# Slot attention in a decoder block: a new order for VectorE and ScalarE in the first part of an iteration

## The chip, the cores and the metric

The kernel runs on one core of a Trainium2 chip. The metric is the device time of one execution in microseconds (us), median over runs. Five engines work side by side and meet at semaphores: TensorE (PE in the profile; PEld is its weight load), VectorE (DVE), ScalarE (ACT), GpSimd (POOL) and SyncE (SP), which issues transfers. Each engine works off its own instructions in the order in which they are written, so an instruction that waits holds up all that stand behind it on its engine.

## The reference

The block has three parts: decay attention with an MLP, cross-attention with three rounds of slots and a GRU, and a routed mixture of experts. Only the second is touched. Its core, with 2048 slots of width 256 and 1601 context rows:

```python
k_proj = einsum('bmd,ed->bme', Pn, Wk);  v_proj = einsum('bmd,ed->bme', Pn, Wv)
for _ in range(3):
    sn = rmsnorm(slots, slot_norm_w)
    q = einsum('bkd,ed->bke', sn, Wq)
    scores = einsum('bkd,bmd->bkm', q, k_proj) * scale
    attn = softmax(scores, axis=-2)                      # over the slots
    attn = attn / (sum(attn, axis=-1, keepdims=True) + EPS)
    updates = einsum('bkm,bmd->bkd', attn, v_proj)
    slots = gru_cell(updates, slots, gru_wi, gru_wh, gru_bi, gru_bh)
```

## The kernel before

Everything of this part is in `cross_attention`, one program written out by hand for each engine, with a loop over three iterations `it`. The keys and queries are folded beforehand, so that scores are the context (`kq_hi`, `kq_lo`) times the slots (`s_hi`, `s_lo`). Numbers are held as a rounded part and a remainder (`hi`, `lo`), and each product is three matmuls (`three_pass`, lines 76 to 78).

The 1601 context rows make 13 tiles `m` (`MT`), of 128 rows each but the last, which has 65. The 2048 slots make four chunks `c` of 512 columns. A score block (m, c) is six matmuls of 512 columns into one PSUM bank. In the main loop two banks are used in turn (`score_bank`), so a block may start only when the block two places before has been read out. The first four tiles (`AHEAD`) are the `lead`: their 16 blocks have an order of their own, and PE uses three banks there.

What happens to a tile:

- **scaling** (VectorE, L838, `scale_scores`): reads the bank, multiplies, writes `x_e` (chunks 0 to 2) or `x_E` (chunk 3) and takes a maximum. It frees the bank. `negated` (L844) then gives the tile's maximum to ScalarE.
- **exponentials** (ScalarE, L766 for chunks 0 to 2, L768 for chunk 3), with their sums.
- **inverse** (VectorE, L855 and L856, two tiny instructions), which waits for both exponentials.
- **normalised copies** (ScalarE, L771 for chunks 0 to 2, L772 for chunk 3), which wait for the inverse.
- **high parts** (ScalarE, L749 into `p_hi`, one for each of chunks 0 to 2) and **low parts** (VectorE, L850 into `p_lo`). A high part of tile m waits until the update of tile m-2 has read the slot that it takes.
- **sums** (VectorE, L868, for tile 0 the copies L865): they add the tile to `x_acc`, chunks 0 to 2 at once (`sum_weights(m, 0)`) and chunk 3 (`sum_weights(m, 1)`).
- **update** (PE): six matmuls for each chunk 0 to 2, with `p_lo` and `p_hi` as moving data. They need the low part.

PE's order in the main loop is: four score blocks of tile m, then the three updates of tile m-4. After the scores of tile 12 come the updates of tiles 8 to 12, then in a tail the updates of chunk 3 for all tiles, with the row sums (`x_acc` times ones, L1047) after the third of them.

`e` holds four tiles, so the scaling of (m, 0) waits for the sum of tile m-4 and for its last low part. On VectorE, before, `tile_lo(m)` puts a tile's two sums and three low parts in one piece, behind all four scalings of a later tile. The inverse of tiles 1 to 3 comes late: that of tile 2 behind `tile_lo(1)`, that of tile 3 behind `tile_lo(2)` and ahead of `tile_lo(3)`. On ScalarE each tile goes exponentials, both copies, high parts; the same holds for the last two.

## Time and profile before

| | us |
|---|---|
| median of 3 runs | 1453.31 |
| lowest, highest | 1444.6, 1454.62 |
| the profiled execution | 1452.9 |
| its span | 1451.2 |
| PE busy | 1259.7 (87%) |
| VectorE busy | 917.4 (63%) |
| ScalarE busy | 688.9 (47%) |

The profile is a record of one execution. Times within it count from the start of the span. The part that the change touches stands in it three times, roughly at 325 to 500, 568 to 742 and 810 to 984 us. A pause in square brackets is idle time of the engine right before an instruction, with what ended it. The ends of matmuls are modelled, so that neighbouring rows overlap; the distance between two starts is what one of them costs.

### The profile page before, as it was taken

What the parts mean: (1) busy time and instruction counts of PE and PEld (TensorE: products, weight loads), DVE (VectorE), ACT (ScalarE), POOL (GpSimd) and SP (SyncE); (2) the same over time, 40 slices, a digit from 0 to 9 for tenths busy, and PEclk for the clock granted to TensorE, in tenths of its full rate; (3) what the DMA queues carried; (4) which work ended last, traced back from release to release, by engine and by line L of the source; (5) the groups of instructions that cost most, each with busy time, mean ns of one, the idle gap of its engine ahead of it and who ended that gap; (6) DMA issues with size and microseconds to landing.
All of it is one profiled execution on the core that took longest, in us unless ns stands there. A gap on an engine that the chain in (4) does not pass through costs nothing. (4 is left out here: it accounts for less than half of the span.)

```text
span 1451.2 us, 19688 instructions
## 1 busy us (share of the span) xinstructions
PE 1259.7 (87%) x6374; PEld 1043.4 (72%) x6374; DVE 917.4 (63%) x2022; ACT 688.9 (47%) x1219; POOL 291.7 (20%) x366
## 2 busy tenths in 40 slices
PE   3898799659899999989999989999963999999960
PEld 3456688437687788767787868778753999999960
DVE  4325766456786466777546777745466777777747
ACT  4112323154567333656643366653341777777734
POOL 5703200020000000000000000000004566666633
PEclk9999899778999999999899989989955999999985
DMA  5000000500000100000000000006091111111134
GB/s 194 1 0 1 0 19 26 173 20 1 1 0 1 30 8 16 1 1 1 0 30 16 8 1 0 1 15 247 1 342 51 38 43 43 43 43 43 43 121 133
DMA packets 44904, 63.73 MB, mean 44 GB/s; under 512 B 7136, under 2 KB 35745, under 8 KB 44449
## 3 DMA queue, kind: packets, MB, share of 16 engines
q1 hardware_dynamic: 38148, 48.00, 10.1%
q0 software_dynamic: 4416, 12.06, 2.7%
q10 hardware_dynamic: 2272, 2.81, 0.5%
q8 instruction: 37, 0.61, 0.2%
q14 instruction: 31, 0.25, 0.1%
HBM read 50.47 MB, written 12.39 MB: 43 GB/s over the span
## 5 line engine op out<-in xcount | busy, mean ns | idle before, releaser
L76 PE MATMUL x_psum<-x_s_lo,x_kq_hi 128*128 128x512 f32 (+1 forms) x312 | 131.9, 423 | 23.1 <-DVE x_mx L838 21.3
L707 POOL TENSOR_TENSOR x_sq<-x_sq 128x512 f32<-128x512 f32 x12 | 15.5, 1289 | 617.2 <-ACT x_sq L693 617.2
L76 PE MATMUL x_psum<-x_p_lo,x_v_hi 128*128 128x512 f32 (+1 forms) x312 | 130.3, 418 | 3.6 <-DVE x_p_lo L850 3.6
L78 PE MATMUL x_psum<-x_p_hi,x_v_hi 128*128 128x512 f32 (+1 forms) x312 | 128.9, 413 | 0.0
L77 PE MATMUL x_psum<-x_p_hi,x_v_lo 128*128 128x512 f32 (+1 forms) x312 | 128.9, 413 | 0.0
L77 PE MATMUL x_psum<-x_s_hi,x_kq_lo 128*128 128x512 f32 (+1 forms) x312 | 127.9, 410 | 0.0
L78 PE MATMUL x_psum<-x_s_hi,x_kq_hi 128*128 128x512 f32 (+1 forms) x312 | 127.3, 408 | 0.0
L838 DVE CUSTOM_DVE_ANT_0 x_e<-x_psum,x_rsb,x_rs 128x512 f32<-128x512 f32 (+1 forms) x117 | 86.3, 748 | 46.7 <-PE x_psum L78 45.8
L76 PE MATMUL e_bank<-e_w_lo,e_g_hi 128*128 128x256 f32 x368 | 107.6, 292 | 0.1
L76 PE MATMUL e_bank<-e_xT_lo,e_w_hi 128*128 128x256 f32 x368 | 105.4, 287 | 1.4 <-DVE e_xT_lo L1729 1.4
L77 PE MATMUL e_bank<-e_xT_hi,e_w_lo 128*128 128x256 f32 x368 | 105.2, 286 | 0.0
L78 PE MATMUL e_bank<-e_xT_hi,e_w_hi 128*128 128x256 f32 x368 | 105.1, 286 | 0.0
L77 PE MATMUL e_bank<-e_w_hi,e_g_lo 128*128 128x256 f32 x368 | 104.1, 283 | 0.0
L78 PE MATMUL e_bank<-e_w_hi,e_g_hi 128*128 128x256 f32 x368 | 104.1, 283 | 0.0
L749 ACT ACTIVATE x_p_hi<-x_e 128x512 fp32r<-128x512 f32 (+1 forms) x117 | 69.7, 625 | 59.0 <-PE x_psum L78 59.0
L76 PEld LDWEIGHTS x_psum<-x_s_lo,x_kq_hi 128*128 128x128 f32 (+1 forms) x312 | 60.8, 195 | 42.1 <-DVE x_mx L838 23.9
L771 ACT ACTIVATE x_e<-x_e,x_inv 128x1536 f32<-128x1536 f32 (+1 forms) x39 | 61.6, 1580 | 58.9 <-DVE x_inv L856 58.9
L1699 ACT ACTIVATE sT<-e_bank,b 128x256 f32<-128x256 f32 x184 | 76.9, 469 | 19.2 <-PE e_bank L78 19.2
L850 DVE TENSOR_TENSOR x_p_lo<-x_e,x_p_hi 128x512 fp32r<-128x512 f32 (+1 forms) x117 | 78.9, 687 | 6.9 <-ACT x_p_hi L749 4.7
L1743 DVE TENSOR_TENSOR e_w_lo<-w,e_w_hi 128x512 fp32r<-128x512 f32 x92 | 66.0, 718 | 27.0 <-ACT e_w_hi L1693 14.1
L1755 DVE TENSOR_TENSOR e_g_lo<-sT,e_g_hi 128x512 fp32r<-128x512 f32 x92 | 63.7, 693 | 28.3 <-ACT e_g_hi L1704 20.3
L76 PEld LDWEIGHTS x_psum<-x_p_lo,x_v_hi 128*128 128x128 f32 (+1 forms) x312 | 62.0, 199 | 20.9 <-DVE x_p_lo L850 5.0
(356 smaller groups left out, 3370.1 us busy)
## 6 DMA issues: line engine op xcount, KB each, us to landing
w<-in_w SPq DMA_DIRECT2D x16, 1024.0 KB, 12.7
w<-scratch_results SPq DMA_DIRECT2D x8, 512.0 KB, 8.2
x_rsb<-scratch_thin_inv SPq DMA_DIRECT2D x12, 256.0 KB, 3.8
x_rsb<-scratch_thin_rs SPq DMA_DIRECT2D x9, 256.0 KB, 3.8
a_x<-in_x SPq DMA_DIRECT2D x1, 2048.0 KB, 12.1
sT<-in_xT ACTq DMA_DIRECT2D x1, 2048.0 KB, 12.3
scratch_x<-a_h SPq DMA_DIRECT2D x4, 512.0 KB, 2.9
r_x<-scratch_x SPq DMA_DIRECT2D x4, 512.0 KB, 6.5
```

The source lines that it names most:

```text
L76: pe.matmul(out, w_hi, x_lo, start=start, stop=False)
L77: pe.matmul(out, w_lo, x_hi, start=False, stop=False)
L78: return pe.matmul(out, w_hi, x_hi, start=False, stop=stop)
L707: pool.tensor_tensor(sq[:, 0], sq[:, 0], sq[:, 1], ALU.add).then_inc(sum_ok, 1)
L749: act.activation(p_hi[0:n, slot], src, ACT.Copy).then_inc(p_hi_ok, 1)
L771: act.activation(e[0:n, m % AHEAD], e[0:n, m % AHEAD], ACT.Copy, scale=inv[0:n, m, 2:3]).then_inc(p32_ok, 1)
L838: v.tensor_tensor_reduce(out, bank[score_bank(i)][0:n], rsb[0:n, chunk(c)], rs16[0:n, m:m + 1], -3.0e38, ALU.mult, ALU.max, mx[0:n, m % AH ...
L850: v.tensor_tensor(p_lo[0:n, slot], src, p_hi[0:n, slot].bitcast(F32), ALU.subtract).then_inc(p_lo_ok, 1)
L1699: act.activation(g32[f % 2][:, a], bank[1 + f % 2][:, a * SLOTS:(a + 1) * SLOTS], ACT.Gelu, bias=b1[:, bass.ds(ex * FT + (2 * f + a), 1)]) ...
L1743: v.tensor_tensor(w2_lo[:, 2 * f:2 * f + 2], w2[:, bass.ds(ex, 1), 2 * f:2 * f + 2].rearrange("p e c f -> p (e c) f"), w2_hi[:, 2 * f:2 * ...
L1755: v.tensor_tensor(g_lo[:, 2 * f:2 * f + 2], g32[f % 2], g_hi[:, 2 * f:2 * f + 2].bitcast(F32), ALU.subtract).then_inc(g_lo_ok, 1)
```

## The change

PE's, SyncE's and GpSimd's instructions and their order stay as they are, and so does the work of VectorE and ScalarE: the same instructions stand in another order.

- In the lead, the first low part of tile 0 moves ahead of the scaling of (3, 3), and the inverse of tile 1 ahead of the others; the sum of chunk 3 of tile 0 moves behind the scaling of (4, 0).
- In tile 4, the inverse of tile 2 comes right behind `negated(4)`.
- From tile 5 on, a scaling of chunk c follows one low part of tile m-3; the inverse of tile m-2 stands behind the second scaling, for tile 3 also; the sums of tile m-3 follow at the end. (Before, from tile 6 on, it was tile m-2's sums and low parts.)
- The waits ahead of a scaling go by chunk: (m, c) waits for the low part of (m-4, c) only. The semaphore `p32_ok` becomes two, one for chunks 0 to 2 and one for chunk 3.
- At the end ScalarE takes the exponentials of tiles 11 and 12 together, then the large copy and the high parts of 11, the same of 12, and both chunk-3 copies last. VectorE has the inverse of 12 ahead of the low parts of 11, and the last sums behind the low parts of 12.

```diff
@@ ScalarE
+                for m in range(MT - 2):
+                    exponentials(m)
+                    normalised(m, 0)
+                    normalised(m, 1)
+                    tile_hi(m)
+                for m in range(MT - 2, MT):
+                    exponentials(m)
+                for m in range(MT - 2, MT):
+                    normalised(m, 0)
+                    tile_hi(m)
+                for m in range(MT - 2, MT):
+                    normalised(m, 1)
@@ VectorE, scale_scores
-                    elif c == 0:
-                        v.wait_ge(acc_ok, (it * MT + m - AHEAD) * 2 + 1)
-                        v.wait_ge(p_lo_ok, it * NP + (m - AHEAD + 1) * KEEP)
+                    elif c < KEEP:
+                        if c == 0:
+                            v.wait_ge(acc_ok, (it * MT + m - AHEAD) * 2 + 1)
+                        v.wait_ge(p_lo_ok, it * NP + (m - AHEAD) * KEEP + c + 1)
@@ VectorE, the order
+                    if (m, c) == (3, 2):
+                        lo(0, 0)
+                sum_weights(0, 0)
+                inverse(1)
+                lo(0, 1)
+
+                lo(0, 2)
+                scale_scores(place_of[(AHEAD, 0)])
+                sum_weights(0, 1)
+                scale_scores(place_of[(AHEAD, 1)])
+                scale_scores(place_of[(AHEAD, 2)])
+                lo(1, 0)
+                scale_scores(place_of[(AHEAD, 3)])
+                negated(AHEAD)
+                inverse(2)
+                sum_weights(1, 0)
+                lo(1, 1)
+                lo(1, 2)
+                sum_weights(1, 1)
+                for m in range(AHEAD + 1, MT):
                     for c in range(NC):
+                        if c < KEEP:
+                            lo(m - 3, c)
                         scale_scores(place_of[(m, c)])
-                        if m == AHEAD and c == 0:
-                            inverse(1)
-                        if m > AHEAD + 1 and c == 1:
+                        if c == 1:
                             inverse(m - 2)
                     negated(m)
-                    tile_lo(m - 3 if m < AHEAD + 2 else m - 2)
-                    if m < AHEAD + 2:
-                        inverse(m - 2)
-                    if m == AHEAD + 1:
-                        tile_lo(m - 2)
-                for m in range(MT - 2, MT):
-                    inverse(m)
-                    tile_lo(m)
+                    sum_weights(m - 3, 0)
+                    sum_weights(m - 3, 1)
+
+                for c in range(KEEP):
+                    lo(MT - 3, c)
+                inverse(MT - 2)
+                sum_weights(MT - 3, 0)
+                sum_weights(MT - 3, 1)
+                inverse(MT - 1)
+                for c in range(KEEP):
+                    lo(MT - 2, c)
+                sum_weights(MT - 2, 0)
+                for c in range(KEEP):
+                    lo(MT - 1, c)
+                sum_weights(MT - 2, 1)
+                sum_weights(MT - 1, 0)
+                sum_weights(MT - 1, 1)
```

In the rows below, which give an engine's instructions in the order of the program, "ISA x_e" is a scaling (its second row, `x_mx`, reads out the maximum), x_p_lo a low part, x_acc a sum, and x_inv with TENSOR_TENSOR and RECIPROCAL the inverse; a number in a name is only a suffix.

VectorE from the last scaling of the lead, (3, 3), to the scaling of (4, 0), before:

```order
L838 ISA x_E_2648,x_mx<-x_psum,x_rsb,x_rs_2640 128x512
L838 ISA x_mx 128x1
L844 TENSOR_REDUCE x_inv<-x_mx 128x1
L865 COPY x_acc<-x_e 128x1536
L850 TENSOR_TENSOR x_p_lo<-x_e,x_p_hi 128x512 x2
L865 COPY x_acc<-x_E_2648 128x512
L850 TENSOR_TENSOR x_p_lo<-x_e,x_p_hi 128x512
L838 ISA x_e,x_mx<-x_psum,x_rsb,x_rs_2640 128x512
```

The same place of the changed kernel, one low part earlier:

```order
L870 TENSOR_TENSOR x_p_lo<-x_e,x_p_hi 128x512
L858 ISA x_E_2648,x_mx<-x_psum,x_rsb,x_rs_2640 128x512
L858 ISA x_mx 128x1
L864 TENSOR_REDUCE x_inv<-x_mx 128x1
L885 COPY x_acc<-x_e 128x1536
L875 TENSOR_TENSOR x_inv<-x_mx 128x1
L876 RECIPROCAL x_inv<-x_inv 128x1
L870 TENSOR_TENSOR x_p_lo<-x_e,x_p_hi 128x512 x2
L858 ISA x_e,x_mx<-x_psum,x_rsb,x_rs_2640 128x512
```

Between the two scalings stood a large copy, three low parts and a small copy; now the small copy and one low part are out and the inverse of tile 1 is in.

VectorE from the scaling of (5, 3) to that of (6, 0), before:

```order
L844 TENSOR_REDUCE x_inv<-x_mx 128x1
L868 TENSOR_TENSOR x_acc<-x_acc,x_e 128x1536
L850 TENSOR_TENSOR x_p_lo<-x_e,x_p_hi 128x512 x2
L868 TENSOR_TENSOR x_acc<-x_acc,x_E_2648 128x512
L850 TENSOR_TENSOR x_p_lo<-x_e,x_p_hi 128x512
L855 TENSOR_TENSOR x_inv<-x_mx 128x1
L856 RECIPROCAL x_inv<-x_inv 128x1
L868 TENSOR_TENSOR x_acc<-x_acc,x_e 128x1536
L850 TENSOR_TENSOR x_p_lo<-x_e,x_p_hi 128x512 x2
L868 TENSOR_TENSOR x_acc<-x_acc,x_E_2648 128x512
L850 TENSOR_TENSOR x_p_lo<-x_e,x_p_hi 128x512
L838 ISA x_e,x_mx<-x_psum,x_rsb,x_rs_2640 128x512
```

And after the change, up to the scaling of (6, 1):

```order
L864 TENSOR_REDUCE x_inv<-x_mx 128x1
L888 TENSOR_TENSOR x_acc<-x_acc,x_e 128x1536
L888 TENSOR_TENSOR x_acc<-x_acc,x_E_2648 128x512
L870 TENSOR_TENSOR x_p_lo<-x_e,x_p_hi 128x512
L858 ISA x_e,x_mx<-x_psum,x_rsb,x_rs_2640 128x512
L858 ISA x_mx 128x1
L870 TENSOR_TENSOR x_p_lo<-x_e,x_p_hi 128x512
L858 ISA x_e,x_mx<-x_psum,x_rsb,x_rs_2640 128x512
```

Two whole tiles of sums and low parts (2 and 3), with the inverse of tile 3 between them, stood ahead of the scaling of (6, 0); now the sums of tile 2 and one low part do, and the inverse of tile 3 stands at (5, 1).

ScalarE, the last two tiles (65 rows mark tile 12), before:

```order
L766 ACTIVATE x_e,x_mx<-x_e,x_inv 128x1536
L768 ACTIVATE x_E_2648,x_mx<-x_E_2648,x_inv 128x512
L771 ACTIVATE x_e<-x_e,x_inv 128x1536
L772 ACTIVATE x_E_2648<-x_E_2648,x_inv 128x512
L749 ACTIVATE x_p_hi<-x_e 128x512 x3
L766 ACTIVATE x_e,x_mx<-x_e,x_inv 65x1536
L768 ACTIVATE x_E_2648,x_mx<-x_E_2648,x_inv 65x512
L771 ACTIVATE x_e<-x_e,x_inv 65x1536
L772 ACTIVATE x_E_2648<-x_E_2648,x_inv 65x512
L749 ACTIVATE x_p_hi<-x_e 65x512 x3
```

And after:

```order
L767 ACTIVATE x_e,x_mx<-x_e,x_inv 128x1536
L769 ACTIVATE x_E_2648,x_mx<-x_E_2648,x_inv 128x512
L767 ACTIVATE x_e,x_mx<-x_e,x_inv 65x1536
L769 ACTIVATE x_E_2648,x_mx<-x_E_2648,x_inv 65x512
L776 ACTIVATE x_e<-x_e,x_inv 128x1536
L750 ACTIVATE x_p_hi<-x_e 128x512 x3
L776 ACTIVATE x_e<-x_e,x_inv 65x1536
L750 ACTIVATE x_p_hi<-x_e 65x512 x3
L776 ACTIVATE x_E_2648<-x_E_2648,x_inv 128x512
L776 ACTIVATE x_E_2648<-x_E_2648,x_inv 65x512
```

The exponentials of tile 12 moved ahead of the copies of tile 11, and the two small copies (chunk 3) behind everything.

## Rows read from the trace of the kernel before

**Rows 1.** The page: the span, and PE's busy time, share and instructions.

```profile
span 1451.2 us, 19688 instructions
PE 1259.7 (87%) x6374; PEld 1043.4 (72%) x6374; DVE 917.4 (63%) x2022; ACT 688.9 (47%) x1219; POOL 291.7 (20%) x366
```

**Rows 2.** PE's waits: line, releaser, us in total, times, longest.

```profile
PE x_psum L76 <- DVE x_mx L838: 21.3, 6, 4.9
PE x_psum L76 <- DVE x_p_lo L850: 3.6, 3, 1.2
```

**Rows 3.** PE in time: start us, duration us, instruction, [idle before <- releaser].

```profile
358.30 0.80 PE L76 MATMUL x_psum<-x_s_lo,x_kq_hi 128*128 128x512 f32 x1 [2.17 <-DVE x_mx L838]
358.89 0.63 PE L77 MATMUL x_psum<-x_s_hi,x_kq_lo 128*128 128x512 f32 x1
359.32 0.63 PE L78 MATMUL x_psum<-x_s_hi,x_kq_hi 128*128 128x512 f32 x1
...
378.96 0.40 PE L77 MATMUL x_psum<-x_s_hi,x_kq_lo 128*128 128x512 f32 x1
379.19 0.39 PE L78 MATMUL x_psum<-x_s_hi,x_kq_hi 128*128 128x512 f32 x1
384.50 0.80 PE L76 MATMUL x_psum<-x_s_lo,x_kq_hi 128*128 128x512 f32 x1 [4.92 <-DVE x_mx L838]
...
464.47 0.40 PE L78 MATMUL x_psum<-x_p_hi,x_v_hi 128*128 128x512 f32 x1
466.09 0.50 PE L76 MATMUL x_psum<-x_p_lo,x_v_hi 65*128 65x512 f32 x1 [1.22 <-DVE x_p_lo L850]
```

**Rows 4.** Stretches: us, busy time (x instructions) of each engine, PEclk, DMA.

```profile
358.22:361.63 3.41, 3.33 (x8) 2.67 (x9) 1.28 (x7) 3.08 (x4) 0.00 (x0) 0.50 0.00 0
382.11:388.94 6.83, 4.44 (x11) 3.47 (x11) 4.00 (x11) 4.09 (x6) 0.00 (x0) 0.50 0.00 1
467.44:477.68 10.24, 10.24 (x26) 7.92 (x25) 3.59 (x6) 3.20 (x4) 0.00 (x0) 0.50 0.00 0
163.70:266.00 102.30, 91.39 (x597) 82.15 (x595) 66.73 (x181) 25.81 (x40) 0.00 (x0) 1.00 0.05 16
```

**Rows 5.** PE in time, in the MLP before: one of three such pauses.

```profile
192.13 0.50 PE L76 MATMUL a_bank<-a_hT_lo,a_w_hi 128*128 128x512 f32 x1 [1.43 <-ACT a_g L316]
```

**Rows 6.** VectorE in time, at the end of the lead.

```profile
354.22 0.95 DVE L865 COPY x_acc<-x_e 128x1536 f32<-128x1536 f32 x1
...
357.48 0.75 DVE L838 CUSTOM_DVE_ANT_0 x_e<-x_psum,x_rsb,x_rs 128x512 f32<-128x512 f32 x1 [0.17 <-DVE x_p_lo L850]
```

**Rows 7.** VectorE in time, from tile 2's sum to the scaling of (6, 0).

```profile
373.54 1.76 DVE L868 TENSOR_TENSOR x_acc<-x_acc,x_e 128x1536 f32<-128x1536 f32 x1
...
377.62 0.15 DVE L855 TENSOR_TENSOR x_inv<-x_mx 128x1 f32<-128x1 f32 x1
377.80 0.16 DVE L856 RECIPROCAL x_inv<-x_inv 128x1 f32<-128x1 f32 x1
379.61 1.76 DVE L868 TENSOR_TENSOR x_acc<-x_acc,x_e 128x1536 f32<-128x1536 f32 x1 [1.64 <-ACT x_e L771]
381.29 1.29 DVE L850 TENSOR_TENSOR x_p_lo<-x_e,x_p_hi 128x512 fp32r<-128x512 f32 x2
383.69 0.74 DVE L838 CUSTOM_DVE_ANT_0 x_e<-x_psum,x_rsb,x_rs 128x512 f32<-128x512 f32 x1
```

**Rows 8.** ScalarE in time: the exponential of tile 3 and the copy that waits.

```profile
371.91 1.56 ACT L766 ACTIVATE x_e<-x_e,x_inv 128x1536 f32<-128x1536 f32 x1
...
378.00 1.58 ACT L771 ACTIVATE x_e<-x_e,x_inv 128x1536 f32<-128x1536 f32 x1 [3.72 <-DVE x_inv L856]
```

**Rows 9.** ScalarE in time, tiles 11 and 12.

```profile
452.85 1.56 ACT L766 ACTIVATE x_e<-x_e,x_inv 128x1536 f32<-128x1536 f32 x1
...
454.40 0.71 ACT L768 ACTIVATE x_E<-x_E,x_inv 128x512 f32<-128x512 f32 x1
...
457.73 1.66 ACT L749 ACTIVATE x_p_hi<-x_e 128x512 fp32r<-128x512 f32 x3
```

30 lines of the change are left out of this document (14 added, 16 removed).

## The prediction

> **What bounds the kernel now.** I read the page first: PE is busy 87% of the span, VectorE 63%, ScalarE 47% [rows 1]. PE's work isn't touched (its instructions and their order are the same), so the change can only give back time in which PE stands idle, or works at its lower clock, in the three iterations. Next I read PE's waits. In this part it waits for a scaling (L838) 6 times, 21.3 us in all, and for a low part (L850) 3 times, 3.6 us [rows 2]. The timeline of PE shows where: in the first iteration 2.17 us before block (4, 2), 4.92 us before (6, 2), 1.22 us before the update (12, 0) [rows 3]. Six is two for each iteration and three is one, so the other two iterations repeat this.
>
> Third, the clock. After each of these pauses a stretch has a granted clock of 0.50, which is 1.2 instead of 2.4 GHz: 3.41 us with 3.33 of them busy, 6.83 with 4.44 busy, 10.24 all busy [rows 4]. At 2.4 GHz the next matmul starts 0.23 us later (378.96, 379.19), at 1.2 GHz 0.43 (358.89, 359.32) [rows 3]. So each loses 0.194 us at the lower level (0.427 less 0.233, the same two distances taken over a dozen matmuls each).
>
> **What each pause is, and what the new order makes of it.** An instruction's successor on VectorE starts 0.08 us before its printed end (379.61 + 1.76 against 381.29 [rows 7]), so a large sum costs 1.68, a low part 0.60 (1.29 for two that overlap by 0.08, [rows 7]), the large copy of tile 0 0.87 [rows 6]. A small sum has a low part's columns and is taken at 0.60. The inverse costs 0.34 (377.62 to 377.96 [rows 7]).
>
> *(4, 2).* Before, the large copy starts at 354.22 and the scaling of (4, 0), which frees the bank, at 357.48 [rows 6]; PE goes on at 358.30. Now the copy (0.87), the inverse of tile 1 (0.34) and two low parts (1.20) stand there: 354.22 + 2.41 = 356.63, the scaling ends 0.75 later at 357.38, PE starts 0.06 later at 357.44. Gain 0.86 us; a pause of about 1.3 stays. The low part of (0, 0) goes ahead of the scaling of (3, 3), where VectorE waits for PE's block anyway.
>
> *(6, 2).* Before, the sum of tile 3 waits 1.64 us for its copy on ScalarE [rows 7], which itself sat idle 3.72 us until the inverse of tile 3 came at 377.96, though that tile's exponentials had begun at 371.91 and take 2.3 us [rows 8, 9]. Behind that sum stand its low parts, and only then the scaling of (6, 0) at 383.69 [rows 7]. The wait is a ring: late inverse, late copy, late sum, late scaling. Now the inverse of tile 2 comes right behind `negated(4)`, which lets ScalarE start that tile's copies 3 us earlier, and the inverse of tile 3 comes with scaling (5, 1), about 371, against 377.96. Between the scalings of (5, 3) and (6, 0) VectorE has the sums of tile 2 and one low part: from 373.54 [rows 7] 1.68 + 0.60 + 0.60 gives 376.4. Block (6, 0) is complete 1.4 us (six matmuls) before (6, 1), whose last starts at 379.19: 379.19 + 0.39 - 1.40 = 378.2 [rows 3]. So the scaling starts at once, ends at 378.95, and (6, 2) can start at 379.0, where PE wants it at 379.42. The whole distance from 379.42 to 384.50, 5.08 us, goes.
>
> *Tiles 5 to 12.* A low part and a scaling together cost 0.60 + 0.67 = 1.27 against 1.40 for six matmuls. With the inverse behind it the second slips by 0.2; the bank has 0.4 to spare (a scaling's 0.75 and two hand-overs of 0.03 and 0.06 against 1.40 less the 0.16 by which the last matmul's end lags the next start). I cost it at nothing; that cover of 0.4 is what to watch.
>
> *Update (12, 0).* ScalarE starts the exponentials of 11 at 452.85; those of 12 follow and end near 457.5 (each tile 1.56 and 0.71 with the read-out, 2.3) [rows 9]. Copy of 11 1.5, its high parts 0.52 each (1.66 for three, [rows 9]): first at 459.6, low part 460.3. PE comes to update (11, 0) at 464.70 less three updates of 1.40, 460.5, so only 0.2 spare; before, this high part stood at 457.73. Copy of 12 from 460.5 to 462.0, high part 462.6; VectorE has the large sum of 11 until 463.2 and the low part until 463.9, and PE wants it when the last matmul of tile 11 is through, at 464.47 + 0.23 = 464.70 [rows 3]. The pause 464.70 to 466.09, 1.39 us, goes. Behind the three low parts (465.1) three sums cost 2.9, then the tail's first low part: 468.6, where PE, with 18 matmuls of 0.233, comes at 468.9. Again 0.3 spare.
>
> Sum of the pauses: 0.86 + 5.08 + 1.39 = 7.3 us an iteration, 22.0 us in three.
>
> **The clock.** Matmuls at 1.2 GHz per iteration: 3.33, 4.44 and 10.24 us at 0.427 are 7.8, 10.4 and 24.0. At 0.194 they lose 1.5, 2.0 and 4.7 us, 8.2 an iteration, 24.6 in three. Do they come back? The pauses that the clock fell after are 4.92, 2.17 and 1.22 [rows 3]. In the MLP, PE has three pauses of about 1.43 us between full matmuls [rows 5], and from 163.7 to 266 the clock stays at 1.00 [rows 4]. The 1.3 that is left of the first is nearer to these: I take it that the clock holds there. The third fell after only 1.22 us, and around that pause run the matmuls of tile 12, which use 65 of 128 rows. It also stayed at 1.2 GHz for 10.24 us of unbroken work, where after the second 4.4 us of full matmuls brought it back [rows 4]. So narrow matmuls count for less; but narrow and pause together made it fall, and the pause goes. I take it that it holds there too.
>
> The Trainium skill (TensorE: Matmul & The Clock Gate, What's actually happening) says the gate is set by how busy PE has recently been, half rate being the idle state. By busy time alone the third stretch should not have stayed at half rate for 10.24 us, as the trace has it; the trace decides. By the page, with the pause gone nothing would lower the clock in the tail and the sum would stand at 1406; by the row, narrow matmuls alone might, and it would be 1420.
>
> **Sum.** 1452.9 (the profiled execution; span 1451.2 [rows 1]) - 22.0 - 24.6 = 1406.3. The profiled execution lies 0.4 under the median of the runs, so no correction is made. Forecast: **1406 us**.
>
> **Rivals.**
>
> *The tail's clock still falls.* For it: 65-row matmuls for 4.2 us in a row, and the lower level held through them before. Against it: it fell only once a pause had come among them. The third stretch stays: 24 x 0.194 x 3 = 14.0, giving 1420; in one or two iterations 1411 to 1416. If the first also stays (7.8 x 0.194 x 3 = 4.5) 1425; that one alone 1411. Chance 0.25.
>
> *The clock isn't tied to these pauses* and all three stretches only move: 1452.9 - 22.0 = 1431. Against it: three of three stretches follow a pause. Chance 0.05.
>
> *New short waits.* The margins of 0.2 before update (11, 0), 0.3 before the tail and 0.4 at every scaling are read from durations to 0.1. If the first two fail by 0.5 us each, 3 us come back; if a pause of over 1 us comes at (11, 0), the tail's clock goes with it: 1406 + 3 + 14 = 1423. Chance 0.09.
>
> *Slower than before.* The low part now ahead of each scaling holds it up. It waits for its high part, and that for the update of tile m-2; if this comes late, the scaling, the bank and PE wait. Place: 8 tiles x 4 scalings x 3 = 96 times. By the sums above a high part (released by the update of its slot) is there about 1 us before its low part is reached. To eat all 46.6 us, each of the 96 would have to be late by 0.49 beyond the 0.4 spare: a low part and scaling of 2.2 instead of 1.27. From that point on it is slower; at 1.2 us late beyond the spare, 1406 + 115 = 1521. Nothing in the rows is that long. Chance 0.03.
>
> **How the numbers follow.** Forecast 0.58, tail 0.25, short waits 0.09, untied clock 0.05, slower 0.03. About 1% (14.5 us) is what a measurement of this kernel tells from no change. Faster by over 1% (under 1438.8) are the first four but for a part of the short waits: 0.94; within 1% 0.04; slower 0.02. The range: down, the runs before reach 8.7 us under their median, which gives 1398; up, the tail's 1420 and a little: 1398 to 1422, which holds the forecast and nearly all of the tail, 0.8.
>
> **What would show it.** Right: PE's waits for a scaling in this part down to three of about 1.3 us, none before (6, 2), none for a low part; ScalarE's wait of 3.7 us before its copies gone; granted clock 1.00 from the lead to the end of the GRU. Wrong: pauses of PE at every second block of the main loop (the 0.4 was not there); a pause before (11, 0) or the first tail update; a stretch of 0.50 while tile 12's updates run without one. It would be far off if PE's pauses went but its time with them did not, that is, if the row sums or the inverse rows' trip through memory, which starts after the tail's third update, ended last: they move with that update, and PE's work behind it is the same, so I cost them at nothing.

## The result and the profile after

The changed kernel takes 1405.93 us (median of 4 runs, 1405.56 to 1406.21), the kernel before 1450.07 in the runs beside it (1444.60 to 1454.62). The ratio is 0.9697, with a 95% interval of 0.9657 to 0.9737: faster by 3.0%. The profiled execution takes 1405.81 us, against 1452.9 of the one before: 47.1 us less, where the terms of the forecast add up to 46.6. Some executions of these kernels are 13 to 38 us shorter than their others (the last section tells of them); none of the changed kernel's, and none of the four of the kernel before, is one of these.

The page of the changed kernel, which answers to [rows 1], with the granted clock in 40 slices of the span (a digit is tenths, and 9 is 90% or more):

```profile
span 1404.0 us, 19742 instructions
PE 1233.4 (88%) x6374; PEld 1026.8 (73%) x6374; DVE 910.3 (65%) x2022; ACT 689.8 (49%) x1219; POOL 290.0 (21%) x366
PEclk9999899878999999999999999999856999999985
```

PE has the same 6374 matmuls and is busy 26.3 us less (1259.7 against 1233.4). 25.0 of these lie in the three iterations: PE is busy 691.5 us from 330.9 to 1051.1 before, and 666.5 us from 330.2 to 1006.0 now. The matmuls are the same ones, and what differs in the rows is the granted clock. From the lead of the first iteration to the end of the third's GRU the page has a 9 in every slice, and the row of that whole stretch (columns as in [rows 4]) gives 1.00:

```profile
330.00:1000.00 670.00, 664.91 (x2826) 529.62 (x2826) 458.56 (x936) 363.20 (x523) 10.36 (x8) 1.00 0.06 20
```

664.91 of 670 us busy leaves 5.1 for all idle time of three iterations. PE's waits, which answer to [rows 2], have one row left for this part, three of 1.2 us, and none for a low part:

```profile
PE x_psum L76 <- DVE x_mx L858: 3.7, 3, 1.2
```

PE in time at the one pause that is left, before (4, 2), as in [rows 3], and at the same place in the second iteration:

```profile
355.25 0.40 PE L78 MATMUL x_psum<-x_s_hi,x_kq_hi 128*128 128x512 f32 x1
356.88 0.50 PE L76 MATMUL x_psum<-x_s_lo,x_kq_hi 128*128 128x512 f32 x1 [1.23 <-DVE x_mx L858]
...
583.35 0.50 PE L76 MATMUL x_psum<-x_s_lo,x_kq_hi 128*128 128x512 f32 x1 [1.24 <-DVE x_mx L858]
```

The distance of these two, 226.47 us, is the length of an iteration. The third comes as long after, at 809.82. Before, the same block starts at 358.30, 600.50 and 842.87, so an iteration took 242.2 and 242.4 us. That is 15.8 us more, where the forecast has 7.3 + 8.2 = 15.5.

VectorE in time around it (as in [rows 6]), and then at the place where it had waited for the copy of tile 3 (as in [rows 7]). The new lines are: scaling L858, low part L870, inverse L875, large copy L885, sums L888.

```profile
353.75 0.95 DVE L885 COPY x_acc<-x_e 128x1536 f32<-128x1536 f32 x1
354.61 0.15 DVE L875 TENSOR_TENSOR x_inv<-x_mx 128x1 f32<-128x1 f32 x1
354.88 1.27 DVE L870 TENSOR_TENSOR x_p_lo<-x_e,x_p_hi 128x512 fp32r<-128x512 f32 x2
356.07 0.75 DVE L858 CUSTOM_DVE_ANT_0 x_e<-x_psum,x_rsb,x_rs 128x512 f32<-128x512 f32 x1
...
370.62 1.76 DVE L888 TENSOR_TENSOR x_acc<-x_acc,x_e 128x1536 f32<-128x1536 f32 x1
372.29 0.69 DVE L888 TENSOR_TENSOR x_acc<-x_acc,x_E 128x512 f32<-128x512 f32 x1
372.89 0.69 DVE L870 TENSOR_TENSOR x_p_lo<-x_e,x_p_hi 128x512 fp32r<-128x512 f32 x1
375.31 0.75 DVE L858 CUSTOM_DVE_ANT_0 x_e<-x_psum,x_rsb,x_rs 128x512 f32<-128x512 f32 x1 [1.73 <-PE x_psum L78]
```

Before, VectorE came to the scaling of (6, 0) late, at 383.69, and PE waited 4.92 us for it. Now VectorE is ready for that scaling 1.73 us before PE has finished the block: the one that waits has changed. ScalarE's copy of tile 3, which answers to [rows 8], waits 0.55 us where it had waited 3.72:

```profile
368.01 1.58 ACT L776 ACTIVATE x_e<-x_e,x_inv 128x1536 f32<-128x1536 f32 x1 [0.55 <-DVE x_inv L876]
```

The tail, VectorE first and then PE. Each low part stands beside the matmul that needs it:

```profile
449.53 1.90 DVE L870 TENSOR_TENSOR x_p_lo<-x_e,x_p_hi 128x512 fp32r<-128x512 f32 x3 [1.50 <-ACT x_p_hi L750]
453.01 1.88 DVE L870 TENSOR_TENSOR x_p_lo<-x_e,x_p_hi 65x512 fp32r<-65x512 f32 x3
457.69 1.88 DVE L870 TENSOR_TENSOR x_p_lo<-x_E,x_p_hi 128x512 fp32r<-128x512 f32 x3
...
450.40 0.40 PE L76 MATMUL x_psum<-x_p_lo,x_v_hi 128*128 128x512 f32 x1
454.61 0.40 PE L76 MATMUL x_psum<-x_p_lo,x_v_hi 65*128 65x512 f32 x1
458.80 0.40 PE L76 MATMUL x_psum<-x_p_lo,x_v_hi 128*128 128x512 f32 x1
```

The first low part of tile 11 ends at 449.53 + 0.69 = 450.2 (0.69 is one low part, 372.89 above); PE takes it at 450.40. That of tile 12 ends at 453.70, 0.9 us before 454.61. The tail's first ends at about 458.4, PE takes it at 458.80.

### The profile page after: what moved, and what is told of

Read it like the earlier page. It is cut to its first block and busy times, and to the rows that moved or that the text cites. A ratio compares the mean times of both kernels' runs of the same rounds, so it can differ in the third digit from the quotient of the medians.

```text
span 1404.0 us, 19742 instructions
## 1 busy us (share of the span) xinstructions
PE 1233.4 (88%) x6374; PEld 1026.8 (73%) x6374; DVE 910.3 (65%) x2022; ACT 689.8 (49%) x1219; POOL 290.0 (21%) x366
## 5 line engine op out<-in xcount | busy, mean ns | idle before, releaser
L76 PE MATMUL x_psum<-x_s_lo,x_kq_hi 128*128 128x512 f32 (+1 forms) x312 | 126.5, 405 | 5.5 <-DVE x_mx L858 3.7
L76 PE MATMUL x_psum<-x_p_lo,x_v_hi 128*128 128x512 f32 (+1 forms) x312 | 124.6, 399 | 0.0
L77 PE MATMUL x_psum<-x_s_hi,x_kq_lo 128*128 128x512 f32 (+1 forms) x312 | 123.9, 397 | 0.0
L78 PE MATMUL x_psum<-x_s_hi,x_kq_hi 128*128 128x512 f32 (+1 forms) x312 | 123.6, 396 | 0.0
L78 PE MATMUL x_psum<-x_p_hi,x_v_hi 128*128 128x512 f32 (+1 forms) x312 | 123.5, 396 | 0.0
L77 PE MATMUL x_psum<-x_p_hi,x_v_lo 128*128 128x512 f32 (+1 forms) x312 | 123.4, 396 | 0.0
L858 DVE CUSTOM_DVE_ANT_0 x_e<-x_psum,x_rsb,x_rs 128x512 f32<-128x512 f32 (+1 forms) x117 | 86.4, 747 | 50.0 <-PE x_psum L78 49.1
L870 DVE TENSOR_TENSOR x_p_lo<-x_e,x_p_hi 128x512 fp32r<-128x512 f32 (+1 forms) x117 | 78.1, 682 | 5.8 <-ACT x_p_hi L750 5.8
L76 PEld LDWEIGHTS e_bank<-e_xT_lo,e_w_hi 128*128 128x128 f32 x368 | 71.6, 195 | 2.5 <-DVE e_xT_lo L1772 1.8
```

The costliest lines, as they stand in the source:

```text
L76: pe.matmul(out, w_hi, x_lo, start=start, stop=False)
L77: pe.matmul(out, w_lo, x_hi, start=False, stop=False)
L78: return pe.matmul(out, w_hi, x_hi, start=False, stop=stop)
L858: v.tensor_tensor_reduce(out, bank[score_bank(i)][0:n], rsb[0:n, chunk(c)], rs16[0:n, m:m + 1], -3.0e38, ALU.mult, ALU.max, mx[0:n, m % AH ...
L870: v.tensor_tensor(p_lo[0:n, slot], src, p_hi[0:n, slot].bitcast(F32), ALU.subtract).then_inc(p_lo_ok, 1)
```

## The experiments

Two theories stood against each other. **Theory 1** is that of the forecast: three pauses, each with its own cause, and behind each a stretch at the lower clock that goes with it. For the pause before (6, 2) it names the late inverses. **Theory 2** says that the pause before (6, 2) comes from VectorE having the work of two tiles in a row there, whatever the inverses do. Beside these stood whether the clock falls for a pause or for the matmuls of tile 12, which use 65 of 128 rows. In the expectations "theory" and "rival" mean what each of them says itself.

Each kernel is compared with the changed kernel, 1405.93 and in a later set 1405.47, or, where it starts from the kernel before, with that kernel beside it. Chips: the first four below ran on one, the next four on a second, the last four on a third. The changed kernel ran beside the last four alone.

The column "part" is read from the profiled execution: the us from the first score matmul of the first iteration to the first matmul into `r_bank`, behind the third iteration. It leaves out what differs from execution to execution ahead of and behind the iterations. For the kernel before it is 725.7, for the changed one 677.9: 47.8 us less.

| kernel | starts from | median us | runs | lowest to highest | part |
|---|---|---|---|---|---|
| tail_old | changed | 1419.87 | 4 | 1411.46 to 1420.52 | 691.9 |
| batched | changed | 1405.44 | 4 | 1403.12 to 1406.77 | 678.0 |
| narrow_twice | changed | 1417.67 | 4 | 1417.24 to 1419.72 | 690.6 |
| lead_new_order | changed | 1401.92 | 4 | 1387.53 to 1402.79 | 674.3 |
| early_inverses | before | 1436.88 | 10 | 1424.30 to 1440.14 | 708.2 |
| put_off | before | 1443.28 | 4 | 1405.05 to 1444.38 | 715.4 |
| pause_narrow | changed | 1410.40 | 4 | 1409.04 to 1410.51 | 683.7 |
| pause_wide | changed | 1409.69 | 4 | 1379.41 to 1411.63 | 681.9 |
| after_again | (changed) | 1405.47 | 6 | 1403.38 to 1406.61 | 677.2 |
| new_order_again | changed | 1401.16 | 6 | 1387.71 to 1403.11 | 674.2 |
| lead_old | changed | 1416.51 | 5 | 1397.94 to 1418.39 | 688.4 |
| late_inverses | changed | 1417.02 | 4 | 1416.34 to 1418.10 | 688.2 |

### The tail in its old order

```diff
@@ ScalarE
-                for m in range(MT - 2):
+                for m in range(MT):
                     exponentials(m)
...
-                for m in range(MT - 2, MT):
-                    exponentials(m)
-                for m in range(MT - 2, MT):
-                    normalised(m, 0)
-                    tile_hi(m)
-                for m in range(MT - 2, MT):
-                    normalised(m, 1)
@@ VectorE, behind lo(MT - 3, c)
-                inverse(MT - 2)
                 sum_weights(MT - 3, 0)
                 sum_weights(MT - 3, 1)
-                inverse(MT - 1)
...
+                for m in range(MT - 2, MT):
+                    inverse(m)
+                    sum_weights(m, 0)
+                    lo(m, 0)
+                    lo(m, 1)
+                    sum_weights(m, 1)
+                    lo(m, 2)
```

> The changed kernel (1405.9 us) with the end of the old order: ScalarE takes tiles 11 and 12 one after the other, VectorE has each one's inverse, large sum and low parts in the old order. Theory (the pause before update (12, 0), next to the 65-row matmuls of tile 12, is what lowers PE's clock in the tail): by laying the measured durations along the waits, the pause comes back at 1.4 to 2.0 us, and behind it 24 matmuls at 1.2 GHz cost 4.7 us: 6.1 to 6.7 an iteration, 18 to 20 in three, so 1424 to 1426 us, with a stretch of granted clock 0.50 behind each pause. Rival (the clock's falls were not tied to the pauses): only the pause comes back, 4 to 6 us, so 1410 to 1412 us and a clock of 1.00.

It takes 13.9 us more, and the part 14.0. That is less than the theory had said and more than its rival. PE before (12, 0) in the first two iterations, then at (4, 2) in all three, then three stretches (columns as in [rows 4]): the same place behind the pause of the first, the second and the third iteration.

```profile
457.05 0.50 PE L76 MATMUL x_psum<-x_p_lo,x_v_hi 65*128 65x512 f32 x1 [1.82 <-DVE x_p_lo L863]
685.58 0.70 PE L76 MATMUL x_psum<-x_p_lo,x_v_hi 65*128 65x512 f32 x1 [1.83 <-DVE x_p_lo L863]
...
357.36 0.50 PE L76 MATMUL x_psum<-x_s_lo,x_kq_hi 128*128 128x512 f32 x1 [1.22 <-DVE x_mx L851]
585.88 0.50 PE L76 MATMUL x_psum<-x_s_lo,x_kq_hi 128*128 128x512 f32 x1 [1.24 <-DVE x_mx L851]
819.04 0.50 PE L76 MATMUL x_psum<-x_s_lo,x_kq_hi 128*128 128x512 f32 x1 [1.24 <-DVE x_mx L851]
...
457.00:467.00 10.00, 9.95 (x40) 7.59 (x41) 6.26 (x10) 5.69 (x9) 0.00 (x0) 1.00 0.00 0
685.71:695.95 10.24, 10.24 (x25) 7.94 (x26) 4.12 (x7) 3.72 (x6) 0.00 (x0) 0.50 0.00 0
921.23:928.05 6.82, 6.82 (x18) 5.34 (x17) 1.82 (x4) 3.20 (x4) 0.00 (x0) 0.50 0.01 2
```

The pause came back in all three iterations, but the clock fell behind two of them only. The starts at (4, 2) price both apart. The first iteration, in which the clock held, takes 228.52 us against 226.47: 2.05 for the pause (1.82 idle, and 0.2 since two matmuls no longer overlap). The second, in which it fell, takes 233.16: 4.64 more, and 10.24 us at 0.427 are 24 matmuls that lose 0.194 each, 4.66. In the third 16 matmuls were slow, 3.1. The sum, 3 x 2.05 + 4.7 + 3.1 = 13.9, is what was measured. So the tail's edits are worth what they take away, but the clock's part isn't paid each time: the same pause of 1.8 us has 40 matmuls behind it in 10 us in one iteration and 25 in the next. One of the four runs took 1411.46 us, with a mean granted clock of 0.940 where the others have 0.935 or 0.936. The three pauses alone would give 1412.1; it wasn't profiled, so that the clock held behind all three is likely and not shown.

### The low parts in one piece

```diff
                     for c in range(NC):
-                        if c < KEEP:
-                            lo(m - 3, c)
                         scale_scores(place_of[(m, c)])
...
                     negated(m)
+                    for c in range(KEEP):
+                        lo(m - 3, c)
                     sum_weights(m - 3, 0)
```

> The changed kernel, but from tile 5 on the three low parts of tile m-3 stand in one piece behind the four scalings, ahead of the sums, instead of one by one ahead of the scalings. Theory 1 (what breaks the ring is that tile m-3 and not m-2 is taken, with the inverses early; the one-by-one order is worth nothing): 1406 us within 1.5, no pause of PE in the main loop. Theory 2 (the low parts between the scalings are what lets the scaling of (6, 0) start in time): a pause before (6, 2) comes back, 2 to 5 us an iteration and its stretch of lower clock with 2.0, so 1418 to 1427 us.

1405.44 us, no difference from the changed kernel. PE's waits have the same row, and the stretch (columns as in [rows 4]) the clock of 1.00:

```profile
PE x_psum L76 <- DVE x_mx L858: 3.7, 3, 1.2
333.00:1000.00 667.00, 661.95 (x2815) 526.56 (x2814) 458.67 (x935) 362.55 (x522) 10.34 (x8) 1.00 0.07 21
```

One low part ahead of each scaling costs nothing, as forecast, and it brings nothing: how finely a tile's work is mixed with the scalings doesn't count. Whether it counts which tile's work stands there is asked by put_off and late_inverses below.

### Twice the narrow matmuls

```diff
                     pe.wait_ge(p_lo_ok, it * NP + j + 1)
+                    if m == MT - 1 and c < KEEP:
+                        for h in range(DH):
+                            three_pass(pe, bank[2 + DH * c + h], v_hi[0:n, m, hs(h)], v_lo[0:n, m, hs(h)],
+                                       p_hi[0:n, slot], p_lo[0:n, slot], False, False)
```

> The changed kernel, with each of tile 12's updates of chunks 0 to 2 (65 rows) issued twice on PE, so that tile 12 counts twice in these sums and the output changes; nothing else is altered. It measures whether narrow matmuls without a pause lower the clock. Theory (a pause is needed): 18 matmuls of 0.233 more in each iteration, 12.6 us in three, so 1418.5 us and a clock of 1.00 through the tail. Rival (narrow matmuls alone lower it, and the 4.2 us of them in the changed kernel were just short enough): a stretch of 0.50 around the tail of each iteration, 12.6 and 3 x (3 to 8) us, so 1427 to 1442 us.

This one counts tile 12 twice in its updates. It takes 11.7 us more, and the part 12.7, where 18 further matmuls in each of three iterations, at 0.233, are 12.6. The stretch (columns as in [rows 4]) has a clock of 1.00 throughout:

```profile
332.00:1000.00 668.00, 662.92 (x2819) 527.37 (x2818) 452.31 (x927) 360.05 (x518) 10.36 (x8) 1.00 0.06 20
```

Twice the narrow matmuls in a row, without a pause, don't lower the clock. This is what the tail's rival stood on, and it falls; the changed kernel's own clock of 1.00 had said so for half as many.

### A pause without and with the narrow matmuls

The first makes PE wait for a later sum before update (12, 0), the second for all three low parts of tile 11 before update (11, 0), where the matmuls right around have 128 rows; the narrow ones begin 4.2 us later.

```diff
@@ pause_narrow
                     pe.wait_ge(p_lo_ok, it * NP + j + 1)
+                    if (m, c) == (MT - 1, 0):
+                        pe.wait_ge(acc_ok, (it * MT + MT - 2) * 2 + 2)
@@ pause_wide
                     pe.wait_ge(p_lo_ok, it * NP + j + 1)
+                    if (m, c) == (MT - 2, 0):
+                        pe.wait_ge(p_lo_ok, it * NP + j + 3)
```

> The changed kernel (1405.9 us) with one wait more on PE: update (12, 0), the first with 65 rows, waits for VectorE's small sum of tile 11. That ends at 455.50 in the profile of the changed kernel, and PE would start at about 454.6: a pause of 0.9 to 1.0 us, followed by 65-row matmuls. Theory (pause next to narrow matmuls lowers the clock): 3 us of pauses and a stretch of 0.50 behind at least two of three, so 1416 to 1424 us. Rival (0.9 is too little even there): 1409 us, clock 1.00.

> The changed kernel with one wait more on PE, four matmul groups earlier: update (11, 0), with 128 rows, waits for all three low parts of tile 11, the last of which ends at 451.43, where PE would start at about 450.4: a pause of 1.0 to 1.1 us in the midst of full matmuls. All theories: 3 us of pauses. Theory (a pause this short among full matmuls leaves the clock alone, as the MLP's of 1.43 us did): 1409 us and clock 1.00. Rival (any pause of a microsecond can lower it): 1412 to 1423 us.

4.5 and 3.8 us more than the changed kernel, which didn't run beside them; the part is 5.8 and 4.0 us longer. PE's waits and the stretches (columns as in [rows 4]), pause_narrow first; its second stretch lies in the third iteration, the last line is pause_wide's:

```profile
PE x_psum L76 <- DVE x_acc L888: 2.7, 3, 0.9
454.50:461.00 6.50, 6.49 (x28) 5.28 (x29) 4.63 (x6) 3.95 (x6) 0.00 (x0) 1.00 0.00 0
911.94:918.77 6.83, 6.83 (x18) 5.28 (x17) 2.34 (x4) 2.98 (x4) 0.00 (x0) 0.50 0.01 2
```

```profile
PE x_psum L76 <- DVE x_p_lo L870: 3.0, 3, 1.0
332.00:1000.00 668.00, 659.87 (x2802) 524.23 (x2801) 456.96 (x933) 362.11 (x521) 10.36 (x8) 1.00 0.06 20
```

With the narrow matmuls, the clock fell behind one of three pauses of 0.89 us; without them, behind none of three that are slightly longer. The first expectation missed: it had two falls at least, and 1416 to 1424 us. The second came in as its theory said. One fall in three against none in three doesn't settle whether the narrow matmuls matter; the count over all traces, in the last section, says more.

### The early inverses alone

```diff
-                        if m > AHEAD + 1 and c == 1:
+                        if m > AHEAD and c == 1:
                             inverse(m - 2)
                     negated(m)
-                    tile_lo(m - 3 if m < AHEAD + 2 else m - 2)
-                    if m < AHEAD + 2:
+                    if m == AHEAD:
                         inverse(m - 2)
+                    tile_lo(m - 3 if m < AHEAD + 2 else m - 2)
```

> The kernel before (1450 to 1453 us) with one part of the change alone: the inverse of tile 2 right behind the maximum of tile 4, that of tile 3 behind the second scaling of tile 5; sums and low parts stand as before. Theory 1 (the prediction's reading: the pause of 4.92 us before (6, 2) is a ring that starts with the late inverse): the pause goes or falls under 1 us, and with it the stretch of lower clock, 15 and 6 us in three iterations, so 1430 to 1436 us. Theory 2 (the two tiles of sums and low parts in one piece ahead of the scaling of (6, 0) are long enough by themselves: 373.54 and 2 x 4.08 give 381.7, the scaling ends at 382.4): 3.0 us of it stay, and since the inverse of tile 2 now waits for its exponentials ahead of tile 1's low parts, up to 1.8 us come before (5, 2): within 4 us of the kernel before.

1436.88 us, with the kernel before beside it at 1446.45; but that one's 13 runs lie between 1413.85 and 1456.31, and the times alone leave it unclear. The traces say more: the part takes 708.2 us, 17.5 less than before. PE in the second iteration, and the stretch it lies in (columns as in [rows 4]):

```profile
610.16 0.50 PE L76 MATMUL x_psum<-x_s_lo,x_kq_hi 128*128 128x512 f32 x1 [1.71 <-DVE x_mx L838]
623.11 0.50 PE L76 MATMUL x_psum<-x_s_lo,x_kq_hi 128*128 128x512 f32 x1 [2.92 <-DVE x_mx L838]
596.00:708.00 112.00, 103.97 (x445) 81.76 (x444) 85.24 (x171) 76.42 (x110) 0.00 (x0) 1.00 0.00 1
```

The pause before (6, 2) is 2.92 us where it was 4.92, so two of the five were the ring of the late inverse. That is the length that Theory 2 had laid out for two tiles that follow each other on VectorE, and Theory 1 as the forecast put it falls. In time both missed: Theory 1 had 1430 to 1436, and Theory 2 within 4 us of the kernel before. There's more: a pause before (5, 2) takes 1.71 us in the one iteration in which the clock had held behind (4, 2), and 0.15 to 0.17 in the other two, and the pauses in all are only 4.0 us shorter than before. The rest is clock. In the whole part it stands at the lower level for 23.9 us, where it stood there for 3 x 20.48 = 61.4. In the second iteration it doesn't fall at all, behind pauses of 2.19, 1.71, 2.92 and 1.22 us.

### One tile at a time, inverses as before

```diff
                     negated(m)
-                    tile_lo(m - 3 if m < AHEAD + 2 else m - 2)
+                    tile_lo(m - 3)
                     if m < AHEAD + 2:
                         inverse(m - 2)
-                    if m == AHEAD + 1:
-                        tile_lo(m - 2)
+                tile_lo(MT - 3)
```

> The kernel before with the other part alone: in every tile of the main loop VectorE takes tile m-3's sums and low parts in one piece (never two tiles in a row), the inverses stay late. Theory 2 (two tiles in a row make the pause): no pause before (6, 2); the delay of ScalarE that the late inverses leave comes out later, 1.6 us before (7, 2), and the end, which now has one tile more behind the last scaling, pauses 1.0 us before update (11, 0) and 2.3 before (12, 0): 7.1 us of pauses an iteration against 8.3 (8.6 as laid out), 1 to 5 us less in three and up to 6 more from the middle stretch of the clock: 1442 to 1451 us. Theory 1 (the late inverse makes it): the pause of 3 to 5 us before (6, 2) or (7, 2) stays, 1450 to 1455 us.

1443.28 us, within what its Theory 2 gave. The kernel before stood at 1446.45 beside it, which is too near to tell by the times; the part is 10.3 us shorter than before. PE's waits, and the one that is left of the middle pause, now before (7, 2):

```profile
PE x_psum L76 <- DVE x_mx L838: 11.6, 6, 2.2
PE x_psum L76 <- DVE x_p_lo L850: 8.6, 6, 2.0
392.55 0.50 PE L76 MATMUL x_psum<-x_s_lo,x_kq_hi 128*128 128x512 f32 x1 [1.68 <-DVE x_mx L838]
```

The 4.92 before (6, 2) have become 1.68 a tile later, and the stretch at the lower clock behind them is gone from all three iterations. So from this side the two tiles in a row are 3.2 us of the pause and the late inverses 1.7; from the side of early_inverses they are 2.9 and 2.0. But the tile that is put off has to be done at the end: for low parts PE waits twice in each tail, 0.89 and 1.97 us, where it had waited once, 1.22. Putting off without the new tail moves a part of the wait to the end.

### The inverses late, in the changed kernel

```diff
                 negated(AHEAD)
-                inverse(2)
                 sum_weights(1, 0)
...
                 sum_weights(1, 1)
+                inverse(2)
...
-                        if c == 1:
+                        if c == 1 and m > AHEAD + 1:
                             inverse(m - 2)
...
                     sum_weights(m - 3, 1)
+                    if m == AHEAD + 1:
+                        inverse(m - 2)
```

> The changed kernel with the inverses of tiles 2 and 3 where they were before, behind tile 1's and tile 2's sums and low parts; all else as changed. Theory 1 (both parts are needed, since a late inverse makes ScalarE's copies and high parts late, on which the low parts and sums now wait): 2.1 us before (5, 2) and 0.9 before (6, 2), laid out 3 us an iteration, so 1414 to 1416 us, and up to 6 more where the clock falls. Theory 2 (taking tile m-3 is all that counts): 1406 us, no pause at (5, 2) or (6, 2).

11.5 us more than the changed kernel beside it (1405.47), and the part 10.9 us longer; Theory 1 had 1414 to 1416 and more where the clock falls. PE's waits, and one of three pauses before (5, 2):

```profile
PE x_psum L76 <- DVE x_mx L858: 11.6, 9, 2.0
369.30 0.50 PE L76 MATMUL x_psum<-x_s_lo,x_kq_hi 128*128 128x512 f32 x1 [1.98 <-DVE x_mx L858]
```

Beside the three of 1.2 us there are now 1.98 us before (5, 2) and 0.41 to 0.78 before (6, 2) in each iteration, and one clock stretch of 3.41 us. So in the new order the inverses of tiles 2 and 3, 0.34 us each, keep away pauses of 7.9 us in all: 11.6 less 3.7. Here Theory 2 falls too, in its "whatever the inverses do": it is right that little is left before (6, 2), but the late inverses then hold up (5, 2). Neither the early inverses nor the one tile at a time would do alone; each takes another part of the delay away.

### The lead in its old order

```diff
-                    if (m, c) == (3, 2):
-                        lo(0, 0)
                 sum_weights(0, 0)
-                inverse(1)
+                lo(0, 0)
                 lo(0, 1)
+                sum_weights(0, 1)
                 lo(0, 2)
                 scale_scores(place_of[(AHEAD, 0)])
-                sum_weights(0, 1)
+                inverse(1)
                 scale_scores(place_of[(AHEAD, 1)])
                 scale_scores(place_of[(AHEAD, 2)])
-                lo(1, 0)
                 scale_scores(place_of[(AHEAD, 3)])
...
                 sum_weights(1, 0)
+                lo(1, 0)
                 lo(1, 1)
+                sum_weights(1, 1)
                 lo(1, 2)
-                sum_weights(1, 1)
```

> The changed kernel (1405.9 us) with VectorE's old order up to tile 4: the low parts of tile 0 in one piece with both copies ahead of the scaling of (4, 0), those of tile 1 in one piece with its sums; the inverses of 1 and 2 at (4, 0) and behind the maximum of tile 4. Theory (a late scaling of (4, 0) and what it pushes): the pause before (4, 2) is 2.1 to 2.2 us again, and a second of 1.7 us comes before (5, 2); laid out, the iteration is 2.4 us longer, 7 us in three, and where the clock falls behind the first 1.5 more each: 1413 to 1418 us. Rival (the prediction's term, 0.86 us an iteration and nothing behind it): 1408 to 1409 us, or up to 1413 with the clock.

11.0 us more than the changed kernel beside it, and the part 11.1 us longer. PE's waits, and the stretch at the lower clock in the first iteration, which follows the second pause there (columns as in [rows 4]):

```profile
PE x_psum L76 <- DVE x_mx L858: 8.8, 6, 2.0
353.82:357.23 3.41, 3.41 (x10) 2.62 (x8) 1.87 (x5) 2.19 (x2) 0.00 (x0) 0.50 0.00 0
```

The pause before (4, 2) is back at 1.9 us, and a second one stands before (5, 2): 2.04 us in the iteration where the clock held behind the first, 0.50 and 0.48 in the two where it fell there. With PE slow between the two, VectorE had time to catch up. The forecast gave the lead's edits 0.86 + 1.5 us an iteration, 7.1 in all; taken back alone they cost 11.0. The waits are 5.1 us more than the changed kernel's, 3.0 of them the second pause, which had not been counted, and three stretches of 3.41 us lose 1.5 each. In the profile of before the clock fell behind (4, 2) in all three iterations, which may be why no second pause is to be read there: in early_inverses one of 1.71 us stands in the only iteration in which it held.

### A new lead, and the changed kernel again

The pause that is left has the large copy, the inverse and two low parts ahead of the scaling of (4, 0). This kernel gives the copy a place further up, behind the scaling of (2, 3), and puts the low parts and sums one by one between scalings up to tile 5.

```diff
                         inverse(0)
+                    if (m, c) == (2, LAST):
+                        sum_weights(0, 0)
                     if (m, c) == (3, 2):
                         lo(0, 0)
-                sum_weights(0, 0)
+                scale_scores(place_of[(AHEAD, 0)])
                 inverse(1)
                 lo(0, 1)
-
-                lo(0, 2)
-                scale_scores(place_of[(AHEAD, 0)])
-                sum_weights(0, 1)
                 scale_scores(place_of[(AHEAD, 1)])
+                lo(0, 2)
                 scale_scores(place_of[(AHEAD, 2)])
+                sum_weights(0, 1)
                 lo(1, 0)
...
                 negated(AHEAD)
-                inverse(2)
-                sum_weights(1, 0)
                 lo(1, 1)
                 lo(1, 2)
+                inverse(2)
+                sum_weights(1, 0)
+                scale_scores(place_of[(AHEAD + 1, 0)])
                 sum_weights(1, 1)
+                lo(2, 0)
+                scale_scores(place_of[(AHEAD + 1, 1)])
+                inverse(3)
+                lo(2, 1)
...
```

> The changed kernel with another order of VectorE around the end of the lead: the large copy of tile 0 stands behind the scaling of (2, 3), the scalings of (4, 0) and (4, 1) follow (3, 3) with the inverse of tile 1 and one low part between them, the sums of tiles 0 and 1 lie behind the scalings of (4, 2) and (5, 0). Theory (the pause of 1.24 us before (4, 2) is VectorE's work in a wrong order, which its idle time before (3, 2) and behind (4, 3) can take): the pause goes, nothing takes its place, 1.4 us an iteration, so 1402 us. Rival (VectorE has no room there, and the pause only moves to (4, 3) or (5, 2)): 1405 to 1407 us with a pause of 0.7 to 1.5 us at one of these blocks.

> The kernel with the lead's new order once more beside the changed kernel on the same chip. Theory (the 1.24 us pause goes and 0.17 us of a late first matmul with it, no other comes): 4.2 us under the changed kernel beside it, 1401 to 1403 us. Rival (the first difference was the chip's): within 1 us of it.

> The changed kernel itself once more, on the chip of the runs beside it, as their measure: 1405 to 1407 us, three pauses of 1.24 us before (4, 2), none before (6, 2) or (12, 0), the clock at 1.00 from the lead to the end of the GRU. If the clock's rises and falls shift between executions, as in the kernel with early inverses alone, a stretch of 0.50 may appear behind one of the 1.24 us pauses (1.5 us each).

1401.92 and 1401.16 us; the changed kernel beside the second set 1405.47 (six runs each). That is 4.3 us, 0.3%, under the changed kernel, and the best of all kernels here. If the run of 1387.71 is left out, its five others lie between 1400.25 and 1403.11, all below the six of the changed kernel (1403.38 to 1406.61). PE has no wait for a scaling any more; the stretch (columns as in [rows 4]):

```profile
331.00:997.00 666.00, 664.60 (x2824) 528.08 (x2823) 457.91 (x936) 362.88 (x524) 10.33 (x8) 1.00 0.06 21
```

The gain is the three pauses of 1.23 and little more, as the clock had not fallen behind them: the part is 3.0 us shorter than that of the changed kernel beside it, and 3.6 in the first set.

## Why the prediction was right, point by point

The forecast of 1406 was met to 0.1 us (its sum, 1406.3, to 0.4), and that is luck in part. It starts from one profiled execution at 1452.9, while the kernel before had a median of 1450.07 beside the changed one and of 1446.45 to 1453.32 in the other sets; the terms, 46.6, would have given 1403.5 from the first of these. What holds without luck is the part, 47.8 us shorter where 46.6 had been summed.

- **The pause before (4, 2).** A pause of about 1.3 us should stay: it is 1.23. The copy, inverse and two low parts take 356.07 - 353.75 = 2.32 where 2.41 had been summed, and the scaling's 0.75 follows at once. The size of this term was right as a part of the whole change. As a price of the lead's edits alone it was too small (7.1 against 11.0 in lead_old), since it left out the pause of up to 2 us before (5, 2) that comes with the old order.
- **The pause before (6, 2).** It went in full, as forecast, and the inverse of tile 3 lets ScalarE's copy go with 0.55 us of waiting instead of 3.72. **The step that failed is the cause:** "The wait is a ring: late inverse, late copy, late sum, late scaling" is only 1.7 to 2.0 of the 4.92 us, as put_off and early_inverses show from either side. The other part is that VectorE had tile 3's work straight behind tile 2's, which the change takes apart too. The forecast counted only tile 2's sums and one low part between (5, 3) and (6, 0), and so had this in its numbers, but not in its reason.
- **Tiles 5 to 12 at nothing.** Right: no pause between them in 96 places, and batched shows that the mixing itself is worth nothing either way.
- **Update (12, 0) and the margins.** The pause is gone. Of the spare times forecast, 0.2 us before (11, 0) and 0.3 before the tail, 0.2 and 0.4 were there. Had they failed, pause_narrow and pause_wide give the price: 3.8 to 4.5 us for about a microsecond in each iteration, less than the rival's 17.
- **The clock.** The forecast took all 24.6 us as won, and in the changed kernel the granted clock is 1.00 through all three iterations, 1.23 us pauses included; PE's busy time in this part, 25.0 us less, agrees with 24.6. But that each pause brings its own stretch was read from an execution in which all nine fell. Its iterations are alike: the stretches behind (4, 2) begin at 358.22, 600.56 and 842.91, each 242.3 us behind the last, and the others repeat in the same way, so nine falls are three readings, each taken three times. In the other traces it isn't so: two of three in tail_old, one of three in pause_narrow, none of four in one iteration of early_inverses. The tail's edits were summed at 1.39 + 4.7 an iteration, 18.2 in all; taken back they cost 14.0 for just this reason.
- **The narrow matmuls.** "So narrow matmuls count for less" doesn't follow from the 10.24 us for which the clock stayed down. PE in the kernel before, from the first matmul with 128 rows to the last of that stretch:

```profile
472.82 0.63 PE L76 MATMUL x_psum<-x_p_lo,x_v_hi 128*128 128x512 f32 x1
477.51 0.47 PE L78 MATMUL x_psum<-x_p_hi,x_v_hi 128*128 128x512 f32 x1
```

Twelve of the stretch's 24 matmuls are full ones. They ran at the lower clock for 4.9 us without a break, where behind (6, 2) the clock came back after 4.4 us of them. The choice that was made on it, that with the pause gone the clock holds, came true; the reason for the long stretches stays open.
- **The rival in the tail**, with a chance of 0.25, is refuted by the changed kernel's clock of 1.00 and, with twice the matmuls, by narrow_twice.
- The Trainium skill (TensorE: Matmul & The Clock Gate, What's actually happening) says the gate follows how busy PE has lately been, and that it looks at times of its own, not bound to where a program's matmuls begin. That the same pause lowers the clock in one iteration and not in the next fits the second half. By the first half alone pause_wide, with the longer pauses (1.01 us, no fall), should not do better than pause_narrow (0.89, one fall); one case of three doesn't settle that.

The effects don't add, by the part of each profiled execution: tail_old's 14.0, late_inverses' 10.9 and lead_old's 11.1 are 36.0, and starting from the other side early_inverses brings 17.5 us and put_off 10.3. All edits together bring 47.8. No kernel takes back the one-tile order of the changed kernel alone, so its price from that side wasn't measured.

## What to carry to other kernels

Where an engine with no work to spare waits for another, follow the wait back over all engines until it closes on itself; then ask of each link what else would be late if only that one were mended, since the links are worth little alone. Short operations that release another engine's long one (here 0.34 us of inverse ahead of a 1.6 us copy) belong as early as their inputs allow; mixing the long ones finely with the work that waits brought nothing here. Price a pause by itself first and put the lower clock behind it as a range from nothing to what one profile shows, as whether it falls changes from one iteration to the next. Iterations that repeat each other to 0.1 us are one reading of it, not three.
